# A gated delta-rule attention kernel: a shorter chain of products for the chunk inverse, and the order of the work around it

## The reference

```
q, k, v, z = projections of the mixed x; q, k, v through a 4-tap causal convolution and silu
g = cumsum(-exp(A_log) * softplus(a + dt_bias)) per chunk;  beta = sigmoid(b)
decay = tril(exp(g_i - g_j))
M = strictly lower part of (k_beta @ k.T) * decay
T = solve_triangular(I + M, I)            # the chunk inverse
v_c, k_cumdecay = T @ v_beta, T @ (k_beta * exp(g))
per chunk:  v_new = v_c - k_cumdecay @ state
            out = (q * exp(g)) @ state + ((q @ k.T) * decay) @ v_new
            state = state * exp(g_last) + (k * exp(g_last - g)).T @ v_new
h = norm_w * rmsnorm(out) * silu(z);  result = x + h @ W_out.T  (then the second mixing and the linear layer)
```

## Time and profile before

| | |
|---|---|
| median of 3 runs | 3395.84 us (3394.86 to 3396.92) |
| the profiled execution | 3396.61 us, span of its trace 3394.8 us |
| busy share of the span | PE 94%, weight loads 74%, DVE 74%, ACT 58%, POOL 47% |
| one body | about 48 us, 66 of them |

### The profile page before, as it was taken

How to read it: one execution, slowest core, us unless ns; L and a number is a source line. 1 busy time by engine, 2 the same in 40 slices (tenths; PEclk the granted TensorE clock), 3 DMA queues, 4 the chain that set the end, 5 groups by cost and what they waited for, 6 DMA issues and landing times.

```text
span 3394.8 us, 57303 instructions
## 1 busy us (share of the span) xinstructions
PE 3187.6 (94%) x18210; PEld 2528.4 (74%) x18210; DVE 2510.9 (74%) x5359; ACT 1984.0 (58%) x4832; POOL 1592.0 (47%) x2825
## 2 busy tenths in 40 slices
PE   0149999999999999999999999999999999999999
PEld 0138787878778877887787877787878778877865
DVE  7866777777777777777777777777777777777754
ACT  6735655565566655665566556655565556656652
POOL 7653545445454544445444544545354544545330
PEclk9989999999999999999999999999999999999999
DMA  3322222222222222222232222223222222223222
GB/s 112 124 79 88 84 59 85 81 71 69 81 88 78 78 71 83 71 83 66 84 87 79 60 84 78 81 59 91 82 84 62 82 82 72 80 69 89 71 55 75
DMA packets 296750, 267.79 MB, mean 79 GB/s; under 512 B 221664, under 2 KB 251488, under 8 KB 287200
## 3 DMA queue, kind: packets, MB, share of 16 engines
q1 hardware_dynamic: 287520, 134.09, 15.9%
q10 hardware_dynamic: 8928, 130.03, 10.5%
HBM read 233.35 MB, written 30.67 MB: 78 GB/s over the span
## 4 chain that ended last, share of the span: by engine, by line
PE 91%; DVE 1%; issue 1%; ACT 1%; POOLq 0%; POOL 0%; DVEq 0%; ACTq 0%
PE x L739 31%; PE lane L865 20%; PE x L830 7%; PE rb L759 5%; PE ra L747 4%; PE rc L772 3%; PE rb L830 3%; PE ra L830 3%; PE rc L770 2%; PE ra L748 2%; PE rc L789 2%; PE x L789 2%; PE rb L819 1%; PE x L780 1%; PE rc L796 1%; PE x L892 1%
## 5 line engine op out<-in xcount | busy, mean ns | idle before, releaser
L739 PE MATMUL x<-xs,w_high 128*128 128x512 f32 x3072 | 1056.9, 425 | 20.7 <-DVE attn L1317 7.7
L1020 ACT ACTIVATE uvec<-rb,cpos 128x128 f32<-128x128 f32 x512 | 160.4, 364 | 847.0 <-PE rb L759 847.0
L739 PE MATMUL x<-xs,w_low 128*128 128x512 f32 x1536 | 609.5, 397 | 0.0
L739 PEld LDWEIGHTS x<-xs,w_high 128*128 128x128 f32 x3072 | 526.8, 191 | 85.7 <-issue 12.4
L1124 ACT ACTIVATE slot<-lane 128x512 fp32r<-128x512 f32 x640 | 364.7, 650 | 154.2 <-PE lane L865 154.2
L1512 POOL TENSOR_TENSOR block_step<-block_in 64x14 f32<-64x14 f32 (+6 forms) x896 | 231.4, 258 | 341.3 <-DMA block_in<-blocks_dram 220.0
L739 PEld LDWEIGHTS x<-xs,w_low 128*128 128x128 f32 x1536 | 290.3, 189 | 67.2
L1488 POOL TENSOR_TENSOR lower<-bt,offdiag 128x512 fp32r<-128x512 f32 x128 | 163.3, 1276 | 366.1 <-DVE bt L1311 366.1
L1218 DVE SCALAR_TENSOR_TENSOR cacc<-x,cwv,cacc 128x511 f32<-128x511 f32 (+2 forms) x384 | 281.6, 747 | 37.9 <-ACT cacc L1007 3.3
L1569 POOL TENSOR_TENSOR rstd<-rarg,powers 128x8 f32<-128x8 f32 x64 | 107.0, 1672 | 416.3 <-DVE rarg L1255 416.3
L1218 DVE SCALAR_TENSOR_TENSOR cacc<-x,cwqk,cacc 128x511 f32<-128x511 f32 (+2 forms) x384 | 281.2, 746 | 28.0 <-ACT cacc L1007 6.1
(11 more groups left out here) (299 smaller groups left out, 7460.0 us busy)
## 6 DMA issues: line engine op xcount, KB each, us to landing
xs<-mix_dram ACTq DMA_DIRECT2D x62, 2048.0 KB, 7.7
gb<-cum_dram SPq DMA_DIRECT2D x128, 256.0 KB, 4.3
w_in<-in_w_qkvz SPq DMA_DIRECT2D x48, 512.0 KB, 4.1
w_out<-in_w_out SPq DMA_DIRECT2D x16, 512.0 KB, 5.8
blocks_dram<-bt SPq DMA_DIRECT2D x512, 8.0 KB, 1.5
inverse_dram<-block_out SPq DMA_DIRECT2D x64, 128.0 KB, 2.2
inv<-inverse_dram SPq DMA_DIRECT2D x512, 16.0 KB, 1.9
xacc<-in_x SPq DMA_DIRECT2D x4, 1024.0 KB, 10.1
```

Source lines behind the costliest of these rows:

```text
L739: ins = mm(PROJ_BANK[kind][i][:, :], w, x, start=(k == 0 and j == 0), stop=(k == KC - 1 and j == 2))
L1020: ins = a(uvec[:, h, :], rb[:, sl(h, HD)], ACT.Copy, scale=sm2[p]["cpos"][:, ch, h:h + 1])
```

## The change

The sum of the series is regrouped. With X the product of the off-diagonal part with the block inverse, P = D + X D the first two terms and X2 = X X, the old kernel made X2 in both orientations and X4 from them, and went from P to (I + X2) P and from there to (I + X4)(I + X2) P, which is the same sum; the new one evaluates P + X2 (P + X2 (P + X2 P)), each step a product with s2 and a sum with pinv on VectorE. That is one product and one slot fewer (JOBS 11 to 10, SLOTS 20 to 19). VectorE now has the jobs 2, 4, 5, 6, 8 and 9, ScalarE 0, 1, 3 and 7.

Around it, in the slots' new numbers:

- The second half of the z projection on TensorE goes from slot 11 to slot 10, ahead of the query transposes; the heads' transposes go from slot 10 to slot 11, behind job 2. ScalarE's `silu_z` for it goes with it. The output calls are spread anew.
- VectorE: the strict mask moves from `b_matrix` into `key_sums` (slot 13 to slot 10), `small` from slot 12 to slot 10 right behind; the value `qe` moves out of `small` into `query_sums`, which stays in slot 12. `b_matrix` of head 1 and `add_out` move by a slot.
- ScalarE: `query_squares` moves to slot 11 with the first exponential (chunk 0 of head 0) behind it; the other seven follow in slot 12.
- `out(1, 0)` waits for the squares instead of for the small values; GpSimd and SP wait for other product numbers.

```
--- before.py
+++ after.py
@@ -22,8 +22,8 @@
 ITERS = HQK * BATCH
 EPS = 1e-6
 BLK = 16
-SLOTS = 20
-JOBS = 11
+SLOTS = 19
+JOBS = 10
 FIRST = SLOTS - JOBS
 NB = P // BLK
 
@@ -507,7 +507,7 @@
         block_in = sb("block_in", [NB * HPG * NCH, BLK, BLK])
         block_step = sb("block_step", [NB * HPG * NCH, BLK, BLK])
         block_out = sb("block_out", [NB * HPG * NCH, 2, BLK, BLK], F32R)
-        kks = sq[:, 0, :].rearrange("p (c s) -> p c s", s=CH)
+        kks = sq[:, 1, :].rearrange("p (c s) -> p c s", s=CH)
         attn2 = [sb(f"attn{i}", [P, HPG, NCH, CH]) for i in range(2)]
         slot = [sb(f"slot{i}", [P, HPG, NCH, CH], F32R) for i in range(3)]
         pinv = sb("pinv", [P, HPG, NCH, CH], F32R)
@@ -568,7 +568,7 @@
         added = [sem(f"head{h}_product_added") for h in range(HPG)]
 
 
-        ADDED = (4, 6, 7, 9, 10)
+        ADDED = (2, 4, 5, 6, 8, 9)
         block = c.enter_context(nc.Block())
 
         COL = {"qk": 0, "v": 256, "z": 512}
@@ -645,7 +645,7 @@
                 sp.wait_ge(S["block_stored"], m * 16 + 16)
                 if m > 0:
                     for h in range(HPG):
-                        await_product(sp, m - 1, h, 4)
+                        await_product(sp, m - 1, h, 2)
                 for a in range(NB):
                     rows = slice(a * BLK, (a + 1) * BLK)
                     sp.dma_start(inv16[rows, :, :, :, rows].rearrange("i h c w j -> i (h c w) j").bitcast(F32),
@@ -826,7 +826,7 @@
                     if m is not None:
                         W("z_ready", 2 * m + 2)
                 if (j, h) == (1, 0) and l is not None:
-                    W("sk_ready", l + 1)
+                    W("squares_ready", l + 1)
                 ins = mm(OUT_BANK[j][:, :], w_out[:, h, sl(j, P)], hT[:, h, :], start=(h == 0), stop=(h == HPG - 1))
                 if h == HPG - 1:
                     ins.then_inc(S["op_full"], 1)
@@ -837,12 +837,11 @@
             PRODUCTS = [
                 (lower, natural),
                 (natural, lower),
+                (s0, turned),
                 (s1, s0),
-                (s0, s1),
-                (s0, turned),
-                (lower, s2),
                 (s2, pinv),
-                (s0, pinv),
+                (s2, s0),
+                (s2, s1),
                 (pinv, None),
                 (None, s1),
                 (s2, pinv),
@@ -966,26 +965,25 @@
                         if L:
                             key_products(l, m, p)
                     elif k == 10:
+                        proj("z", 1, 2, 3)
                         if L:
                             query_tokens(l, m, p)
+                    elif k == 11:
                         if B:
                             heads_t(n, m)
-                    elif k == 11:
-                        proj("z", 1, 2, 3)
                     elif k == 12:
                         out(0, 0)
                     elif k == 13:
                         out(0, 1)
                     elif k == 14:
                         out(1, 0)
+                        out(1, 1)
                     elif k == 15:
-                        out(1, 1)
-                    elif k == 16:
                         out(2, 0)
                         out(2, 1)
+                    elif k == 16:
+                        out(3, 0)
                     elif k == 17:
-                        out(3, 0)
-                    elif k == 18:
                         out(3, 1)
 
             LOOP(pe, body)
@@ -1033,14 +1031,15 @@
                 W("qtok_full", l + 1)
                 a(sq[:, 0, :], x1[:, :], ACT.Square).then_inc(S["squares_ready"], 1)
 
-            def exp_decay(l, h):
+            def exp_decay(l, h, chunks):
                 W("gneg_ready", l + 1)
                 if l > 0:
                     W("attn_ready", 2 * l)
                 W("masked", 2 * l + h + 1)
-                for ch in range(NCH):
+                for ch in chunks:
                     ins = a(decay[:, h, ch, :], gb[:, h, sl(ch, CH)], ACT.Exp, bias=sm["gneg"][:, ch, h:h + 1])
-                ins.then_inc(S["decay_ready"], 1)
+                if NCH - 1 in chunks:
+                    ins.then_inc(S["decay_ready"], 1)
 
             def mix_exps(u, k, b):
                 W("mix_clipped", u + 1)
@@ -1146,12 +1145,13 @@
                             silu("qk", l, 0, qkT2[p][:, 1, :])
                         elif k == 8:
                             silu("qk", l, 1, qkT2[p][:, 0, :])
-                        elif k == 10:
+                        elif k == 11:
                             query_squares(l)
+                            exp_decay(l, 0, range(1))
                         elif k == 12:
-                            exp_decay(l, 0)
-                        elif k == 14:
-                            exp_decay(l, 1)
+                            exp_decay(l, 0, range(1, NCH))
+                            exp_decay(l, 1, range(NCH))
+                        elif k == 13:
                             exp_small(l, p)
                     if l == 0 and k == 16:
                         ffn_abs()
@@ -1171,7 +1171,7 @@
                             silu_z(m, 0, q)
                         elif k == 9:
                             copy_vtok(m)
-                        elif k == 11:
+                        elif k == 10:
                             silu_z(m, 1, q)
                             if L and 0 < l < ITERS - 1:
                                 load_input((b + 1) % BATCH)
@@ -1184,7 +1184,7 @@
                             mix_inverse(*mix_unit(l))
 
             s0, s1, s2 = slot
-            DEST = [s0, s1, s2, lower, pinv, s0, pinv, pinv, s1, s2, None]
+            DEST = {0: s0, 1: s1, 3: s2, 7: s1}
             LOOP(act, body)
             ffn_sigmoid(3, 0)
             ffn_sigmoid(3, 1)
@@ -1262,18 +1262,22 @@
                 v.tensor_tensor(work, x0[:, :].rearrange("p (c s) -> p c s", s=CH), ident[:, :].unsqueeze(1).to_broadcast([P, NCH, CH]), ALU.mult)
                 dve.drain()
                 v.tensor_reduce(sums[:, 0, :], work, AX.X, ALU.add)
-
-            def query_sums(l):
+                dve.drain()
+                v.tensor_tensor(kks, x0[:, :].rearrange("p (c s) -> p c s", s=CH),
+                                t["strict"][:, :].unsqueeze(1).to_broadcast([P, NCH, CH]), ALU.mult)
+
+            def query_sums(l, p):
 
                 W("squares_ready", l + 1)
                 v.tensor_reduce(sums[:, 1, :], sq[:, 0, :].rearrange("p (c s) -> p c s", s=CH), AX.X, ALU.add)
+                dve.drain()
+                v.tensor_scalar(qe[p][:, :], sums[:, 1, :], HD * EPS, HD * EPS * HD * EPS, ALU.mult, ALU.add)
 
             def small(m, p):
 
                 dve.drain()
                 W("masked", 2 * m + 2)
                 v.tensor_scalar(skt[:, :], sums[:, 0, :], HD * EPS, None, ALU.add)
-                v.tensor_scalar(qe[p][:, :], sums[:, 1, :], HD * EPS, HD * EPS * HD * EPS, ALU.mult, ALU.add)
                 v.tensor_tensor(sm["edd"][:, :, :], glast[:, :, :],
                                 sm["gct"][:, :, :], ALU.subtract).then_inc(S["sk_ready"], 1)
                 g, b = m // BATCH, m % BATCH
@@ -1301,11 +1305,6 @@
 
             def b_matrix(l, h, p):
 
-                if h == 0:
-                    W("kk_full", l + 1)
-                    v.tensor_tensor(kks, x0[:, :].rearrange("p (c s) -> p c s", s=CH),
-                                    t["strict"][:, :].unsqueeze(1).to_broadcast([P, NCH, CH]), ALU.mult)
-                    dve.drain()
                 W("decay_ready", 2 * l + h + 1)
                 for ch in range(NCH):
                     ins = v.scalar_tensor_tensor(out=pair[p][:, h, ch, :], in0=kks[:, ch, :], scalar=sm["cneg"][:, ch, h:h + 1],
@@ -1321,11 +1320,12 @@
                 for h in range(HPG):
                     dve.wait_ge(prod_full[h], JOBS * m + job + 1)
                     made = lane[h][:, :].rearrange("p (c s) -> p c s", s=CH)
-                    if job == 4:
+                    if job == 2:
                         ins = v.tensor_tensor(pinv[:, h, :, :], made, turned[:, h, :, :], ALU.add)
-                    elif job in (6, 7):
-                        ins = v.tensor_tensor(pinv[:, h, :, :], made, pinv[:, h, :, :], ALU.add)
-                    elif job == 9:
+                    elif job in (4, 5, 6):
+                        dst = {4: s0, 5: s1, 6: pinv}[job]
+                        ins = v.tensor_tensor(dst[:, h, :, :], made, pinv[:, h, :, :], ALU.add)
+                    elif job == 8:
                         ins = v.tensor_tensor(s2[:, h, :, :], made, s1[:, h, :, :], ALU.subtract)
                     else:
                         ins = v.scalar_tensor_tensor(out=pair[q][:, h, :, :], in0=pinv[:, h, :, :], scalar=2.0, in1=made, op0=ALU.mult, op1=ALU.add)
@@ -1443,15 +1443,18 @@
                             elif b == 2:
                                 mix_forward(*mix_unit(l))
                             key_sums(l)
```

(15 more changed lines are left out.)

16 lines of the change are left out of this document (8 added, 8 removed).

## The result

The changed kernel takes 3400.8 us (median of 20 runs, 3395.4 to 3406.9), the kernel before 3396.0 on the same chips (20 runs, 3392.4 to 3397.1). The ratio is 1.0017, 95% interval 1.0010 to 1.0024: slower by 0.1 to 0.24%. The middle of it lies within the 0.2% that I called no change, but on the side that the forecast (3391) didn't point to. It is inside the range. The profiled execution took 3400.0, its span is 3398.2 (before: 3396.6 and 3394.8).

A forecast was written before the change was run, and what follows sets the result against it. TensorE's work was taken as the bound. Of 62 us to be had (57 product, 5 in b = 3), waits for VectorE's gates left 5: 3395.8 - 5 = 3391; own range 3380 to 3401, 8 in 10 3374 to 3405.

The forecast's parts named there:

- Bound and removal: TensorE's work bounds the loop; one product less saves 0.89 us a body, 57 us over 64 bodies.
- The wait: TensorE's first output call waits for VectorE's gates: 0.6 us in b = 0, 3, 1.3 in b = 2, 1.6 in b = 1.
- -5 for the loop and start: Net forecast change: -3 us over 62 bodies, 0.9 saved before the first heads exist, about 0.5 in the last product body.
- The second failed step: the end: In the last body with products but no new keys, a saving of about 0.5 us.
- The story of the cause: Heads' transposes move close to the output call, leaving only job 3 as cover for VectorE; output at 11.02 instead of 9.75 (b = 2).
- Rival 2, the held product: VectorE's small product is held by GpSimd's power, 0.6 us a body, +38 us: 3429; chance 0.08.
- same: Whole-kernel time between the faster (under 3389) and slower (over 3402.6) outcomes; chance 0.42.
- slower: Whole-kernel time over 3402.6, from VectorE's held product or a smaller lengthening of its chain; chance 0.20.
- Edits at nothing: Moved exponentials, query sums, output calls, b matrix and GpSimd's power cost nothing; a late table load at most 0.1 us.
- the early table load: First exponential with table load ahead of ScalarE's job 3 copy: at most 0.1 us late, hidden; uncovered 6 us.
- The 0.33 of b = 3: ScalarE's mixing block ends before the transpose, removing TensorE's residual weight-load wait: 0.33 us every fourth body, 5 us.

The follow-up runs named there:

- experiment 4: Old TensorE and ScalarE order with the shortened chain of ten products, VectorE's gates right behind the key sums, against the kernel before: 3333.8 us, ratio 0.9818.
- experiment 5: The kernel before with six extra constant reductions on VectorE behind the key sums in bodies b = 1 and 2: 3468.9 us, ratio 1.0218.
- experiment 1: The changed kernel with eight unused matmuls ahead of the first output call in bodies b = 1 and 2, against the kernel before: 3389.4 us, ratio 0.9983.
- Experiment 3: The changed kernel with the moves on TensorE and ScalarE undone, VectorE as changed, against the kernel before: 3390.0 us, ratio 0.9984.
- experiment 8: experiment 4 plus b = 3 mixing inverse in slot 16 and the last layer's two VectorE products in slot 18, against the kernel before: 3329.1 us, ratio 0.9807.
- experiment 6: The changed kernel with one extra constant reduction on VectorE behind the small values in every body, against the kernel before: 3458.3 us, ratio 1.0190.
- experiment 2: The changed kernel with mask and small values behind VectorE's gates and query sums behind the fourth sum, against the kernel before: 3385.0 us, ratio 0.9971.

## Why the prediction was right or wrong

**Bound and removal: right.** TensorE's work was the bound; with the cover restored, experiment 4 gains 0.98 us a body where I had 0.89 for the product.

**The wait: right in place, in the chain behind it and in size, to 0.2 us.** First output call behind job 0: 10.36, 11.36, 11.02, 10.36 forecast for b = 0 to 3, 10.18, 11.19, 10.99, 10.18 in the median after. Bodies: 47.70, 48.70, 48.36, 47.70 forecast, 47.48, 48.51, 48.31, 47.49 medians. What the sum of the chain hid is that TensorE stops twice in b = 1 and 2: job 3 already waits, 0.45 and 0.24 us, for the sums of job 2, where I wrote that no other wait would be over 0.1. For b = 0 and 3 I was 0.2 too slow, since the query transposes take 0.36 in their new place (0.46 before) and job 2 is full 0.67 behind its start, where I took 0.70. I put -5 for the loop and start; by the bodies it was -12.

**The step that failed: what the wait does beside lasting.** The sum took TensorE's idle time at its own length. The prediction named no price for the clock at all, although show it at 1.00 in the loop before, which the absence of waits had kept: experiment 5 puts a wait in and the clock falls there too. Six bodies with a low stretch, 10.9 us: this turned -12 into about -1. It also goes with the scatter: experiment 1 takes the stretches away, and its 11 runs lie within 6.8 us instead of 11.5. The Trainium skill (TensorE: Matmul & The Clock Gate, A second HAM failure mode: psum-queue depth-cycling) tells of a bf16 kernel whose TensorE idles for short times between groups of matmuls, often enough for the clock to go back and forth between its two levels, at a cost in throughput. The trace agrees in kind, with 3.41 us at 0.50 behind 1.2 us idle, and shows it for a pair of waits in an otherwise full stream; my text had it in neither sum nor chance.

**The second failed step: the end.** I gave the last body a gain of 0.5. Its own instructions on VectorE (the last layer's products, tied to slot 17) I did not follow through the renumbering. The end is 5.3 us longer. Up to the last product it is 0.5 longer; the wait for the last sum adds 2.0 (3.30 against 1.29); and behind that wait lies a stretch of 6.83 us at the lower clock (3332 to 3339), in which the first hop falls back by another 2.7.

**The story of the cause: half right.** I told the wait as the heads' transposes coming close to their use. Experiment 3 puts them back and the bodies stay as they are. It is the pieces ahead of the gates on VectorE: mask, small values, sums of job 2. The numbers were right because I summed VectorE's chain and not the distance.

**Rival 2, the held product: did not occur.** GpSimd's power now overlaps VectorE's product L1289 in 62 of 64 bodies, and it lasts 0.166 to 0.169 us in each of them. So the rule of the Trainium skill (SBUF — State Buffer, Who interferes with whom), by which a VectorE instruction with two SBUF inputs is held by such a GpSimd instruction for its length, does not show for these operands of 4 and 8 columns; the measurement decides, for this pair. Of the chances, "same" at 0.42 was rightly the largest; but nothing in the 0.20 for "slower" stood for the clock.

**Edits at nothing:** the early table load, the seven exponentials, the query sums and the power cost nothing, as forecast; in the trace TensorE waits for no copy of ScalarE's job 3. The 0.33 of b = 3 did go with the change: b = 3 and b = 0 are equally long. But the reason I gave, one copy of ScalarE less ahead of the transpose, isn't enough: experiment 4 has that too and keeps the 0.3; it takes the earlier exponentials, the wait for the gates as cover, or the mixing's inverse in its later slot (experiment 8).

## What to carry to other kernels

When one engine is full, price a new wait on it twice: for its length, and for what idle time does to its clock; and first look whether the wait's cover can be kept by putting the consumer (here two gates) ahead of work that nobody on the bound engine needs yet. A shortened chain pays in full only if the order of the engines around it is summed again, in each kind of body. Work that is tied to slot numbers moves when slots are taken out, so follow the one-off instructions of the first and last bodies too.

## What the runs showed of the hardware

A granted clock of 0.50 for 3.41 us costs a body about 1.65 us in the changed kernel and 1.5 in experiment 5; 6.83 us of it cost 3.1 to 3.6 (experiment 6). Shortly before it fell, TensorE had been idle for 1.1 to 2.0 us in all. But many bodies with such waits keep the full clock: it falls in 6 of 31 of the changed kernel, in 13 of the 15 b = 1 bodies and no b = 2 body of experiment 5, and never with the single waits of 0.55 us (experiment 2) or where eight matmuls fill 0.9 us of the wait (experiment 1). Executions of one kernel differ by it: of the 20 of the changed kernel the five fastest (3395.4 to 3399.5) have a mean clock of 0.991, the seven over 3403 have 0.988 or 0.989, though some near 3400 have 0.989 as well. What decides which body is hit stays open.
